# Four banks instead of five in layer 2's PSUM ring, and two banks in turn for the replications

## The reference, cut to what matters

```
e  = stack([tbl_f[ids[:, f]] for f in range(39)], axis=1)        # 512 x 39 x 16
xk = x0 = e
for W in (f0, f1, f2):                                            # (39*39 | 128*39) x 128
    z   = einsum('bfd,bgd->bfgd', x0, xk).reshape(b, f * g, d)
    cur = einsum('bpd,pm->bmd', z, W);  outs.append(cur);  xk = cur
z = sum(concatenate(outs, axis=1), axis=-1)                       # 512 x 384
h = relu(concatenate([z, dense_ctx], 1) @ W_top1 + b_top1)        # 400 -> 512
h = relu(h @ W_top2 + b_top2);  y = h @ W_top3                    # 512 -> 256 -> 1
```

## Time and profile before

| | us |
|---|---|
| median of 3 runs | 769.98 (767.8 to 770.18) |
| the profiled execution | 770.37 |
| its span, first to last instruction | 768.6 |
| PE busy | 725.0 (94%) |
| PE weight loads busy | 581.5 (76%) |
| DVE busy | 625.6 (81%) |
| POOL busy | 536.9 (70%) |
| ACT busy | 358.2 (47%) |
| mean granted TensorE clock | 0.989 of full |

### The profile page before, as it was taken

How to read it: one execution, slowest core, us unless ns; L and a number is a source line. 1 busy time by engine, 2 the same in 40 slices (tenths; PEclk the granted TensorE clock), 3 DMA queues, 4 the chain that set the end, 5 groups by cost and what they waited for, 6 DMA issues and landing times.

```text
span 768.6 us, 11565 instructions
## 1 busy us (share of the span) xinstructions
PE 725.0 (94%) x3392; PEld 581.5 (76%) x3392; DVE 625.6 (81%) x1962; ACT 358.2 (47%) x1048; POOL 536.9 (70%) x512
## 2 busy tenths in 40 slices
PE   3999898899999999999999999999999999999977
PEld 3967676678777877778777887778787887877756
DVE  7848889797998579997998479997988479898940
ACT  3225454555554345555553355555553355555421
POOL 6756989897898559897898659874666437585530
PEclk9999999999999999999999999999999999999989
DMA  9350000000000000000000000000000000000000
GB/s 226 62 208 3 4 3 4 3 3 3 2 3 3 2 3 2 4 3 2 4 3 3 3 3 3 3 1 1 1 1 2 1 0 1 1 0 1 2 0 1
DMA packets 12959, 11.15 MB, mean 15 GB/s; under 512 B 3937, under 2 KB 11841, under 8 KB 12643
## 3 DMA queue, kind: packets, MB, share of 16 engines
q1 hardware_dynamic: 8352, 9.24, 4.6%
q0 software_dynamic: 4544, 1.17, 1.4%
HBM read 10.40 MB, written 0.00 MB: 14 GB/s over the span
## 4 chain that ended last, share of the span: by engine, by line
PE 54%; DVE 20%; POOL 14%; issue 8%; ACT 3%; DMA 1%; SPq 0%; DVEq 0%; POOLq 0%; ACTq 0%
DVE scaled L640 14%; PE y L796 9%; PE y L798 9%; PE y L797 8%; PE side L814 5%; POOL emb L341 4%; POOL z_parts L351 4%; PE y L862 3%; PE acc L778 3%; PE side L803 3%; PE acc L772 2%; PE acc L773 2%; DVE z L609 2%; POOL sum L357 2%; POOL sum L364 2%
## 5 line engine op out<-in xcount | busy, mean ns | idle before, releaser
L640 DVE SCALAR_TENSOR_TENSOR scaled<-y,x_rows,scaled 128x128 f32<-128x128 f32 x1728 | 465.6, 342 | 90.0 <-PE y L798 65.1
L467 ACT ACTIVATE scaled<-y,x_rows 128x128 f32<-128x128 f32 x768 | 219.3, 369 | 200.6 <-PE y L798 200.6
L796 PE MATMUL y<-w_hi,x_parts 128*128 128x512 f32 (+1 forms) x640 | 272.6, 426 | 2.0 <-DVE x_parts L615 1.3
L798 PE MATMUL y<-w_hi,x_parts 128*128 128x512 f32 (+1 forms) x640 | 249.3, 389 | 0.0
L797 PE MATMUL y<-w_lo,x_parts 128*128 128x512 f32 (+1 forms) x640 | 249.0, 389 | 0.0
L351 POOL TENSOR_TENSOR z_parts<-z,z_parts 128x512 fp32r<-128x512 f32 x109 | 148.1, 1359 | 84.9 <-ACT z_parts L413 83.8
L341 POOL DMA_INDIRECT emb<-in_tbl_dram,ids_sb x142 | 140.8, 991 | 30.8 <-issue 19.1
L796 PEld LDWEIGHTS y<-w_hi,x_parts 128*128 128x128 f32 x640 | 120.8, 189 | 38.8 <-DVE scaled L640 8.5
L798 PEld LDWEIGHTS y<-w_hi,x_parts 128*128 128x128 f32 x640 | 120.7, 189 | 25.4
L797 PEld LDWEIGHTS y<-w_lo,x_parts 128*128 128x128 f32 x640 | 121.2, 189 | 23.1
L364 POOL TENSOR_TENSOR sum<-sum,scaled 128x512 f32<-128x512 f32 x64 | 82.9, 1296 | 42.7 <-DVE scaled L640 41.4
(11 more groups left out here) (88 smaller groups left out, 536.1 us busy)
## 6 DMA issues: line engine op xcount, KB each, us to landing
w_sb<-in_w_dram SPq DMA_DIRECT2D x1, 2496.0 KB, 8.8
emb<-in_tbl_dram,ids_sb POOLq DMA_INDIRECT x142, 2.3
s_sb<-in_w_dram SPq DMA_DIRECT2D x12, 160.0 KB, 6.1
w_sb<-in_small_tables_dram SPq DMA_DIRECT2D x1, 980.0 KB
wt_sb<-in_W_top_dram SPq DMA_DIRECT2D x1, 768.0 KB, 10.3
s_sb<-in_w_dram SPq DMA_DIRECT2D x4, 144.0 KB, 6.1
diag<-in_selectors_dram SPq DMA_DIRECT2D x1, 532.0 KB
wt_sb<-in_W_top_dram SPq DMA_DIRECT2D x1, 512.0 KB, 11.0
```

Source lines behind the costliest of these rows:

```text
L467: done = act.activation(scaled[:, k % 2, BY_ACT.index(j), i * M:(i + 1) * M], y2[n % RING][:, i * M:(i + 1) * M], ACT.Copy, scale=x0_rows[ ...
L640: dve.scalar_tensor_tensor(part, y2[n % RING][:, i * M:(i + 1) * M], x0_f, part, ALU.mult, ALU.add).then_inc(terms_in, 1)
L796: pe.matmul(dst, x1_hi[:, t % 2, cols], hi, start=True, stop=False)
L798: pe.matmul(dst, x1_lo[:, t % 2, cols], hi, start=False, stop=True).then_inc(y_ready, 1)
```

## The change

Layer 2's ring has four banks, so `layer2(n)` waits for bank n - 4. The bank that this frees becomes a second one for replications: c = -1, 1, 3, 5 use the first (`reps[0]`), c = 0, 2, 4, 6 the second, and replication c of the next tile waits for product c - 2 instead of c - 1; for c = 0 and 1 the copy of c = -1 is enough. The uses of `y2[4]` at the start go to `reps[1]`.

```diff
-RING = 5
+RING = 4
...
-        rep = ps("rep", [P, COLS])
+        reps = [ps("rep_a", [P, COLS]), ps("rep_b", [P, COLS])]
...
-        ids_banks = [rep, acc0, side, y2[4]]
+        ids_banks = [reps[0], acc0, side, reps[1]]
...
         def rest_bank(dq):
-            return (side, y2[4])[dq % 2]
+            return (side, reps[1])[dq % 2]
 
         def rep_bank(u, c):
-            return y2[c % 4] if u == 0 and c >= 0 else rep
+            return y2[c % 4] if u == 0 and c >= 0 else reps[(c + 1) % 2]
...
                         if c >= 0 and c % B_STEP == 0 and c // B_STEP < C0:
                             c = c // B_STEP
-                            if c == 0:
+                            if c < 2:
                                 pe.wait_ge(three_in, t + 2)
                             else:
-                                pe.wait_ge(prod, C0 * (t + 1) + c)
+                                pe.wait_ge(prod, C0 * (t + 1) + c - 1)
                             replicate(t + 1, c)
```

More of the change, by code:

```diff
@@ L433, in first_rows @@
                 copy(x0_rows[:, 0, a:b, :],
-                     (y2[4] if i == 0 else side)[:, 0:(b - a) * FS].rearrange("p (k f) -> p k f", f=FS)).then_inc(rows_in, 1)
+                     (reps[1] if i == 0 else side)[:, 0:(b - a) * FS].rearrange("p (k f) -> p k f", f=FS)).then_inc(rows_in, 1)
             def rows(g, i):
@@ L444, in three @@
                     act.wait_ge(prod, C0 * u)
-                copy(x0_three[:, :], rep[:, :]).then_inc(three_in, 1)
+                copy(x0_three[:, :], reps[0][:, :]).then_inc(three_in, 1)
             def high_part(u, c):
@@ L846, in keep_warm @@
                 for _ in range(n):
-                    pe.matmul(rep[:, :], sel[0:KX, 0:P], sel[0:KX, P:P + COLS], start=True, stop=True)
+                    pe.matmul(reps[0][:, :], sel[0:KX, 0:P], sel[0:KX, P:P + COLS], start=True, stop=True)
             pe.wait_ge(ones_in, 1)
@@ L877, in _ @@
                 replicate(0, c)
-            rows_of(0, y2[4], *FIRST_ROWS[0])
+            rows_of(0, reps[1], *FIRST_ROWS[0])
             pe.wait_ge(w0_hi_in, 1)
```

## The result

The changed kernel takes 774.04 us (median of 17 runs, 770.65 to 776.14) against 770.02 (17 runs), ratio 1.0043 with a 95% interval of 1.0029 to 1.0057: slower by 2.2 to 4.4 us. (The two medians lie 4.0 us apart, the means 3.4.) Forecast were 773.2 us and +3.2. The two profiled executions took 773.45 and 770.37 us, spans 771.6 and 768.6.

What follows compares the result with a forecast made beforehand. PE and DVE were taken to bound the kernel in turns, DVE alone in the last tile. The terms 1.3 + 0.5 + 1.4 = 3.2 us, on the shown median of 769.98, gave 773.2 us; range 770.4 to 777.0.

Steps and rivals of the forecast that it cites:

- The exchange of waits at slot 8: In tiles 2 to 14 the replication's stall of 1.07 us goes, bank 8's of 1.16 comes: 0.10 a tile, 1.3 us.
- Slot 18 in tiles 3, 5, 7, 9: Bank 18 waits for bank 14's additions; each of these four tiles ends 0.13 us later beyond the carry, 0.5 us.
- a carried 0.10: The 0.10 us lost at a tile's start goes through to the rest of the tile and into the next.
- the wait for POOL at slot 28: In tile 5 POOL's release moves only to 313.28 and PE arrives at 313.41; the tile ends 0.23 us later.
- The last tile: ACT's banks start only when the DVE bank four before is added, and DVE pays each delay in full: 1.4 us.
- The links before banks 11, 21, 31, 27 and 37: In the last tile banks 11, 21, 31 lose 0.26, 0.25, 0.3, links between under 0.21; bank 37 starts 1.4 us later.
- Start-up: Four uses of the fifth bank go to the second replication bank, same order and waits: 0.
- A: Rival: the 0.10 is absorbed in each tile, only the last tile pays, 770.3 to 771.4 us; chance 0.28.
- B: Rival: the replication's wait goes, 15.0 us, and the ring's does not take its place, 755 us; chance 0.06.
- C: Rival: bank 6 or 8, late by 0.8 to 1.2, reaches DVE in each tile; price 12.6, 783 us; chance 0.08.
- layer 2's wait for DVE on the weight side: Sign in the table of waits: PE's wait for DVE's additions grows from 8.5 us to about 25.

Runs made afterwards that it cites:

- e7: The kernel before, without the gathers of the second to fourth group of rows; one execution, tiles 2 to 14 1.87 us shorter than before, last tile 32.68.
- e8: The changed kernel, without the gathers of the second to fourth group of rows; one execution, tiles 2 to 14 0.77 us shorter than before, last tile 34.06.
- e4: The changed kernel, but DVE runs each product ahead of the slot's additions; ratio to the kernel before 1.0126.
- e5: The kernel before the change, but DVE runs each product ahead of the slot's additions; ratio to the kernel before 0.9892.
- e6: The changed kernel, but PE runs each replication ahead of the slot's bank group; ratio to the kernel before 1.0015.
- e1: The changed kernel's ring of four banks, but all replications use one bank and wait for the last product; ratio to the kernel before 1.0064.
- e2: The changed kernel, but in the last tile the second replication bank is the ring's fifth; ratio to the kernel before 1.0001, last tile 32.65 us.

## Why the prediction was right, point by point

**The exchange of waits at slot 8**, forecast 13 x 0.10 = 1.3 us: 1.1 by e7 and e8. The mechanism is shown by e4 and e5 (the 0.60 us), e6 (the 0.23) and e1 (the second bank is worth nothing in this order). The mean is 0.085 and not 0.10, as most odd and late tiles pay 0.07 to 0.09; why was not traced. Tile 5 pays only 0.01 and tile 4 0.14: from bank 38 of tile 4 on PE is late by 0.14 to 0.15 where it was 0.09, while DVE stays 0.08 late, so in tile 5, counted from PE's start, DVE is 0.06 earlier.

**Slot 18 in tiles 3, 5, 7, 9**, forecast 0.5: 0.48 by the pairs. In tile 5, counted from its start, PE is 0.54 later behind the block product (forecast 0.61) and 0.17 later behind slot 28 (forecast 0.23, with a carried 0.10 that is 0.03 here). In the changed kernel's tile 5 the wait for POOL at slot 28 is gone, as the forecast had it:

```profile
303.44 0.50 PE L796 MATMUL y<-w_hi,x_parts 128*128 128x512 f32 x1 [0.54 <-DVE scaled L640]
...
313.67 0.39 PE L773 MATMUL acc<-z_parts,w_lo 128*128 128x512 f32 x1
313.90 0.40 PE L778 MATMUL acc<-z_parts,w_hi 128*128 128x512 f32 x1
```

L778 follows at one pitch, where it was held 0.38 before: a wait on POOL hid most of the new one. The prediction booked the extra in the odd tiles; measured from bank 0 to bank 0 it shows in the even one behind (tile 5 +0.02, tile 6 +0.25). PE's last wait, at slot 38, takes the odd tile's end back: bank 38 of tile 5 is 0.16 later than before, bank 39 only 0.03. DVE's last addition of the tile stays 0.16 later, and in tile 6 its addition of bank 4, for which bank 8 now waits, is 0.12 later. The sum of the pair was right, the tile was not.

**The last tile**, forecast 1.4: 1.40, given back in full by e2. The links before banks 11, 21, 31, 27 and 37 show, at 0.28 each; those before banks 24 and 34 don't show at all. The forecast had 0.26, 0.25 and 0.3 for the first three and less than 0.21 for each of the others, so two of the links cost more than forecast and two nothing, and that the sum is exact is in part luck.

**Start-up**, forecast 0: tile 0 begins at 63.61 in place of 63.52, and tiles 0 and 1 together are 0.01 us longer.

**Rivals.** A (absorbed) falls by the lengths of tiles, though a median alone could hardly have told: 1.5 us in 557. B (the freed wait wins, 755 us) falls by the time itself and by the new wait in front of bank 8. C (DVE starves) falls by DVE's rows at bank 4 to 9, which have no gap, and by the even tiles, none of which is longer by more than 0.3.

**What the prediction had wrong** is one of its signs, not a term of the sum: layer 2's wait for DVE on the weight side was to grow from 8.5 to about 25 us, and grew to 43.2, 99 times. The total of a row of waits adds up every held load, those of banks 1, 2, 3, 5 and 6 too: in tile 6 of the changed kernel six loads are held, 2.38 us in sum, and the tile is 0.25 longer. What PE loses goes by the last of them, not by the sum. The span grew by 3.0 us, 1.54 + 1.40 of it in these tiles; the start-up gives the rest (0.09), the tail 0.01.

## What to carry to other kernels

Before a buffer is moved from one ring to another, write down for each wait the event that ends it and the work that stands between the two waits. Here the new wait ended 0.60 us before the old one and had 0.69 us of work behind it, which was the whole balance, and it told that swapping two lines on the reader's side (0.9892) or sharing all banks in program order (0.9905) would gain where moving a bank lost. And a ring's depth must cover the longest way round through another engine: in this kernel, where DVE adds onto what ACT makes, four banks are one too few in the last tile, and that costs 0.28 us at each of five places there. That the diag product hides it elsewhere was argued, not tested.

## What the runs showed of the hardware that had not been expected

DVE's diag product, the same 128 x 640 numbers each time, takes 0.91 us in the median, 2.15 in tile 5 and up to 3.40 in tile 1. Without the later gathers the longest was 1.06. The rows of tile 5 in the kernel before, DVE and then POOL:

```profile
299.62 2.15 DVE L649 TENSOR_TENSOR diag<-x_rows,mask_sb 128x640 f32<-128x640 f32 x1
298.80 0.96 POOL L341 DMA_INDIRECT emb<-in_tbl_dram,ids_sb  x1
299.78 1.30 POOL L364 TENSOR_TENSOR sum<-sum,scaled 128x512 f32<-128x512 f32 x1
301.16 1.22 POOL L366 TENSOR_TENSOR sum<-sum 128x256 f32<-128x256 f32 x1
```

The diag product ends at 301.77, 0.69 behind POOL's addition L364 (301.08). That is a rule here: of the 32 diag products of this trace 29 end 0.68 to 0.69 us behind the end of an addition or subtraction on POOL, whether they take 0.88 or 3.40 us; the other three are the shortest, 0.82. In e7 and e8, without the gathers, it is so for 28 and 27 of 32. So the long ones have waited for POOL's arithmetic, not for the gathers themselves. The reverse shows too. The halving L366 behind it takes 1.22 in place of its median 0.74, and POOL's low part (L351) takes 1.87 in place of 1.30 where the diag product runs first. The five longest diag products (2.15 and more) all begin while a gather is under way, and POOL's next addition or subtraction then goes first. Why it does was not shown.
